# Key and value bias of a slot-attention kernel formed from the unscaled folded weight products, with two weights no longer loaded

## The reference

```python
x_in = _ln(ctx, lnkv_g, lnkv_b)
k = x_in @ wk + bk
v = x_in @ wv + bv
slots = q_mu + jnp.exp(q_logsig) * layernorm(x)
for _ in range(3):
    prev = slots
    q = _ln(slots, lnq_g, lnq_b) @ wq + bq
    attn = softmax(k @ q.T * 16) + 1e-8, normalised over the rows of the context
    slots = (attn.T @ v) @ wu + bu + prev
    slots = gelu(_ln(slots, lnm_g, lnm_b) @ w1 + b1) @ w2 + b2 + slots
    slots = _ln(slots + cond, lnp_g, lnp_b)
x = x + slots
```

## Time and profile before

| what | us |
|---|---|
| median of 3 executions | 339.01 |
| the three | 336.94, 339.01, 339.3 |
| the profiled execution's own time | 339.19 |
| its span, first to last instruction | 337.3 |

### The profile page before, as it was taken

The page is one execution under the profiler, slowest core; times in us unless marked ns, Lnnn a source line. Parts: engine busy times, 40 slices in busy tenths (PEclk is TensorE's granted clock), DMA queues, the critical chain, the costliest instruction groups (busy, mean ns, idle before and its releaser), DMA issues. The chain is left out here.

```text
span 337.3 us, 6560 instructions
## 1 busy us (share of the span) xinstructions
PE 316.9 (94%) x1758; PEld 261.0 (77%) x1758; DVE 292.9 (87%) x851; ACT 235.6 (70%) x563; POOL 202.2 (60%) x385
## 2 busy tenths in 40 slices
PE   8899999999999989999998999799976899999994
PEld 8787888888887878888887788687853577767773
DVE  3699977899899889998999899999998789999874
ACT  2368986967467867785589674855638588898881
POOL 3168966255689764568987547377754944444341
PEclk9999999999999999999999999999999599999999
DMA  7988000000000000000000000000000000000001
GB/s 274 329 320 357 1 1 2 0 0 2 2 0 2 0 2 2 0 3 1 0 2 0 1 2 1 0 3 1 0 2 0 1 34 31 33 31 0 32 34 62
DMA packets 5311, 13.22 MB, mean 39 GB/s; under 512 B 672, under 2 KB 672, under 8 KB 4896
## 3 DMA queue, kind: packets, MB, share of 16 engines
q1 hardware_dynamic: 4160, 10.88, 8.6%
q10 hardware_dynamic: 1120, 1.98, 1.6%
HBM read 10.76 MB, written 2.10 MB: 38 GB/s over the span
## 5 line engine op out<-in xcount | busy, mean ns | idle before, releaser
L290 DVE BATCH_NORM_STATS2 stats<-S 128x6 f32<-128x256 f32 (+1 forms) x112 | 42.0, 416 | 9.3 <-DMA S<-ctx 3.5
L341 PE MATMUL ps_mid<-XT,KT 128*128 128x256 f32 x192 | 46.1, 383 | 3.4 <-ACT XT L357 3.4
L341 PE MATMUL ps_low<-V,PR 128*128 128x257 f32 x192 | 46.2, 383 | 1.7 <-DVE PR L863 1.7
L341 PE MATMUL ps_low<-wn,GT 128*128 128x256 f32 x192 | 45.7, 381 | 0.8 <-ACT GT L639 0.8
L341 PE MATMUL ps_mid<-XT,wt 128*128 128x256 f32 x192 | 45.5, 380 | 0.7 <-ACT XT L357 0.7
L341 PEld LDWEIGHTS ps_low<-V,PR 128*128 128x128 f32 x192 | 36.0, 190 | 8.4 <-DVE PR L863 3.5
L636 ACT ACTIVATE PR<-ps_mid,nmax 128x256 f32<-128x256 f32 x48 | 22.3, 471 | 27.3 <-DVE nmax L873 27.2
L341 PEld LDWEIGHTS ps_low<-wn,GT 128*128 128x128 f32 x192 | 36.1, 190 | 6.7 <-ACT GT L639 1.9
L341 PEld LDWEIGHTS ps_mid<-XT,KT 128*128 128x128 f32 x192 | 34.6, 190 | 8.4 <-ACT XT L357 4.6
L308 POOL TENSOR_TENSOR lnm_ab<-lnm_mv,mhalf 128x2 f32<-128x2 f32 x24 | 17.2, 715 | 38.9 <-DVE lnm_mv L298 38.9
L357 ACT ACTIVATE XT<-ps_t 128x512 f32<-128x512 f32 x56 | 33.1, 591 | 9.2 <-PE ps_t L333 9.2
(11 more groups left out here) (124 smaller groups left out, 706.4 us busy)
## 6 DMA issues: line engine op xcount, KB each, us to landing
S<-ctx SPq DMA_DIRECT2D x8, 256.0 KB, 3.8
X<-x SPq DMA_DIRECT2D x8, 256.0 KB, 3.4
out<-X SPq DMA_DIRECT2D x8, 256.0 KB, 2.0
rowv<-rows SPq DMA_DIRECT2D x1, 1920.0 KB, 9.9
wf<-w_fc_t SPq DMA_DIRECT2D x1, 1024.0 KB, 11.8
wf<-w_proj_t SPq DMA_DIRECT2D x1, 1024.0 KB, 13.8
wt<-w_tr ACTq DMA_DIRECT2D x1, 512.0 KB, 4.2
wn<-w_nat ACTq DMA_DIRECT2D x1, 512.0 KB, 5.8
```

Source lines behind the costliest of these rows:

```text
L290: dve.bn_stats(ln.st[:, at, j, 0:6], tiles[:, j]).then_inc(ln.stats_done, 1)
L341: last = pe.matmul(dst(m), lhs_t[:, c, m * P:(m + 1) * P], rhs[:, c, 0:n], start=(c == 0), stop=(c == 1))
```

## The change

Natural wk and wv are not loaded. ACT, which issued six loads, issues five; SP waits for transposed wv instead of natural wk. ACT copies each of the two products out of PSUM, unscaled, to a new tile `raw`, and DVE folds lnkv_g from there. ACT also spreads lnkv_b and bv over 128 columns each (`spread`, four instructions). All of this stands ahead of ACT's first normalisation. The key bias becomes one accumulation of 8 matmuls, bk with wq and lnkv_b with the raw key product. The value bias becomes one accumulation of 4 matmuls, with the raw value product and wu, and stands in PE's order between the value product and the key product of batch 0. DVE adds bu to it inside batch 0 of the prologue. Two `column` products and the DVE instructions on `ckv` and `bcol` are gone.

```diff
@@ tiles and semaphores
-        wn = sb("wn", [5, C2, D])
+        wn = sb("wn", [3, C2, D])
+        raw = sb("raw", [2, C2, D])
-        bcol = sb("bcol", [C2, P])
+        spread = sb("spread", [2 * C2, P])
-        ckv = sb("ckv", [4, 1])
-        FOLD_CK, FOLD_CV, FOLD_K, FOLD_V, FOLD_ALL = 3, 8, 10, 12, 15
+        FOLD_W, FOLD_K, FOLD_V, FOLD_ALL = 6, 8, 10, 13
@@ sync
-            sp.wait_ge(wk_in, 16)
+            sp.wait_ge(wv_in, 16)
@@ scalar
-            load(wn[:, WK].rearrange("p c d -> p (c d)"), w_nat[0], wk_in)
-            load(wn[:, WV:WU + 1].rearrange("p w c d -> p w (c d)"), w_nat[1:3].rearrange("w p n -> p w n"), wvu_in)
-            load(wt[:, TV].rearrange("p c d -> p (c d)"), w_tr[2], wvu_in)
+            load(wt[:, TV].rearrange("p c d -> p (c d)"), w_tr[2], wv_in)
+            load(wn[:, WU].rearrange("p c d -> p (c d)"), w_nat[0], wu_in)
...
+            def copy_raw(i):
+                act.wait_ge(w_prod, i + 1)
+                act.activation(raw[:, i].rearrange("p c d -> p (c d)"), ps_mid[i][:], ACT.Copy).then_inc(raw_ready, 1)
+
+            act.wait_ge(cols_in, 16)
+            act.wait_ge(consts, 2)
+            for c in range(C2):
+                act.activation(spread[:, c], ones[:], ACT.Copy, scale=col("lnkv_b", c)).then_inc(spread_ready, 1)
+                act.activation(spread[:, C2 + c], ones[:], ACT.Copy, scale=col("bv", c)).then_inc(spread_ready, 1)
+            copy_raw(0)
+            copy_raw(1)
             ln_apply(act, lnc, 0, 0, S[:, 0], XR[:, 0], xc_ready)
@@ vector
-            dve.wait_ge(w_prod, 1)
+            dve.wait_ge(raw_ready, 1)
             for c in range(C2):
-                dve.tensor_scalar(Wkq[:, c], ps_mid[0][:, c * D:(c + 1) * D], col("lnkv_g", c), None,
+                dve.tensor_scalar(Wkq[:, c], raw[:, 0, c], col("lnkv_g", c), None,
                                   ALU.mult).then_inc(w_fold, 1)
-            dve.wait_ge(w_prod, 2)
-            dve.tensor_tensor(ckv[:, 0:2, 0], ps_low[0][:, 0, 0:2], colv[:, COL["bk"]:COL["bk"] + 2],
-                              ALU.add).then_inc(w_fold, 1)
...
+            dve.wait_ge(raw_ready, 2)
+            for c in range(C2):
+                dve.tensor_scalar(Wvu[:, c], raw[:, 1, c], col("lnkv_g", c), None,
+                                  ALU.mult).then_inc(w_fold, 1)
+            rows_x(0, 0)
+            bn_sum(dve, lnx, 0, 0)
             dve.wait_ge(w_prod, 3)
...
-            rows_x(0, 0)
-            bn_sum(dve, lnx, 0, 0)
             dve.wait_ge(bu_in, 16)
-            dve.wait_ge(w_prod, 6)
-            for j in range(J2):
-                dve.tensor_tensor(vbias[:, j], ps_low[1][:, 1, 0:D], row("bu"), ALU.add).then_inc(w_fold, 1)
             dve.wait_ge(sig_ready, 1)
...
+                if isinstance(b, int) and b == 0:
+                    dve.wait_ge(w_prod, 4)
+                    for j in range(J2):
+                        dve.tensor_tensor(vbias[:, j], ps_low[1][:, 1, 0:D], row("bu"), ALU.add).then_inc(w_fold, 1)
+                    dve.wait_ge(w_fold, FOLD_V)
                 dve.wait_ge(low_ready, b + 1)
-                if isinstance(b, int) and b == 0:
-                    dve.wait_ge(w_fold, FOLD_V)
@@ tensor
-            pe.wait_ge(cols_in, 16)
-            pe.wait_ge(wk_in, 16)
-            column(ps_low[0][:, 0], wn[:, WK], lambda c: col("lnkv_b", c)).then_inc(w_prod, 1)
-
-            pe.wait_ge(wvu_in, 32)
+            pe.wait_ge(wv_in, 16)
+            pe.wait_ge(wu_in, 16)
             product(pe, side(ps_mid[1]), wt[:, TV], wn[:, WU]).then_inc(w_prod, 1)
 
-            column(ps_low[0][:, 1], wn[:, WV], lambda c: col("lnkv_b", c)).then_inc(w_prod, 1)
             pe.wait_ge(consts, 5)
             context_t(0, 0)
 
-            pe.wait_ge(w_fold, FOLD_CK)
-            column(ps_low[1][:, 0], wt[:, TQ], lambda c: ckv[:, c]).then_inc(w_prod, 1)
-
-            pe.wait_ge(cv_spread, 2)
-            for c in range(C2):
-                last = pe.matmul(ps_low[1][:, 1, 0:D], bcol[:, c], wn[:, WU, c], start=(c == 0), stop=(c == C2 - 1))
-            last.then_inc(w_prod, 1)
+            pe.wait_ge(cols_in, 16)
+            pe.wait_ge(raw_ready, 1)
+            column(ps_low[1][:, 0], (wt[:, TQ], lambda c: col("bk", c)), (raw[:, 0], lambda c: col("lnkv_b", c)))\
+                .then_inc(w_prod, 1)
+
+            def value_bias():
+                pe.wait_ge(raw_ready, 2)
+                pe.wait_ge(spread_ready, 2 * C2)
+                rhs = [raw[:, 1, c] for c in range(C2)] + [wn[:, WU, c] for c in range(C2)]
+                for i in range(2 * C2):
+                    last = pe.matmul(ps_low[1][:, 1, 0:D], spread[:, i], rhs[i], start=(i == 0), stop=(i == 2 * C2 - 1))
+                last.then_inc(w_prod, 1)
 
             def keys_values(b, u):
                 pe.wait_ge(t_copied, b + (1 + RING))
-                if isinstance(b, int) and b == 0:
-                    pe.wait_ge(w_fold, FOLD_V)
+                if isinstance(b, int) and b < 2:
+                    pe.wait_ge(w_fold, FOLD_K if b else FOLD_W)
                 pe.wait_ge(low_read, 2 * b + 2)
                 product(pe, side(ps_low[u][:, 0]), XT[:, u], Wvu).then_inc(low_ready, 1)
+                if isinstance(b, int) and b == 0:
+                    value_bias()
                 pe.wait_ge(mid_read, 2 * b + 2)
                 product(pe, side(ps_mid[u]), Wkq, XT[:, u]).then_inc(mid_ready, 1)
```

More of the change, by code:

```diff
@@ L118, in col @@
             return colv[:, COL[name] + c:COL[name] + c + 1]
-        WK, WV, WU, W1, W2 = range(5)
+        WU, W1, W2 = range(3)
         TK, TQ, TV = range(3)
@@ L151, in build @@
         wkq_in = sem("wkq_in")
-        wk_in = sem("wk_in")
-        wvu_in = sem("wvu_in")
+        wv_in = sem("wv_in")
+        wu_in = sem("wu_in")
+        raw_ready = sem("raw_ready")
         mlp_in = sem("mlp_in")
@@ L161, in build @@
         w_fold = sem("w_fold")
-        cv_spread = sem("cv_spread")
+        spread_ready = sem("spread_ready")
         sig_ready = sem("sig_ready")
@@ L380, in _ @@
             sp.dma_start(wn[:, W1:W2 + 1].rearrange("p w c d -> p w (c d)"),
-                         w_nat[3:5].rearrange("w p n -> p w n")).then_inc(mlp_in, 16)
+                         w_nat[1:3].rearrange("w p n -> p w n")).then_inc(mlp_in, 16)
             sp.dma_start(rowv[:, ROWS_EARLY:], rows[ROWS_EARLY:].rearrange("(a n) -> a n", a=1)
@@ L680, in _ @@
             dve.wait_ge(cols_in, 16)
-            dve.wait_ge(w_prod, 1)
+            dve.wait_ge(raw_ready, 1)
             for c in range(C2):
-                dve.tensor_scalar(Wkq[:, c], ps_mid[0][:, c * D:(c + 1) * D], col("lnkv_g", c), None,
+                dve.tensor_scalar(Wkq[:, c], raw[:, 0, c], col("lnkv_g", c), None,
                                   ALU.mult).then_inc(w_fold, 1)
-            dve.wait_ge(w_prod, 2)
-            dve.tensor_tensor(ckv[:, 0:2, 0], ps_low[0][:, 0, 0:2], colv[:, COL["bk"]:COL["bk"] + 2],
-                              ALU.add).then_inc(w_fold, 1)
             for c in range(C2):
                 dve.tensor_scalar(kgain[:, c:c + 1], col("lnq_g", c), LOGIT_SCALE, None, ALU.mult).then_inc(w_fold, 1)
-            dve.wait_ge(w_prod, 3)
-            for c in range(C2):
[L692 to L701, removed]
+            dve.wait_ge(raw_ready, 2)
[4 more added lines that the diff above has]
+            bn_sum(dve, lnx, 0, 0)
+            dve.wait_ge(w_prod, 3)
             for c in range(C2):
@@ L743, in w1_fold @@
                     dve.tensor_scalar(W1g[:, c], wn[:, W1, c], col("lnm_g", c), None, ALU.mult).then_inc(w_fold, 1)
-                dve.wait_ge(w_prod, 7)
+                dve.wait_ge(w_prod, 5)
                 dve.tensor_tensor(b1fold[:], ps_low[0][:, 1, 0:2], colv[:, COL["b1"]:COL["b1"] + 2],
@@ L947, in _, with column @@
             pe.sem_inc(mid_ready, RING)
-            def column(dst, w, v):
+            def column(dst, *pairs):
                 for m in range(C2):
-                    for c in range(C2):
-                        last = pe.matmul(dst[:, m:m + 1], w[:, c, m * P:(m + 1) * P], v(c),
-                                         start=(c == 0), stop=(c == C2 - 1))
+                    for i, (w, v) in enumerate(pairs):
+                        for c in range(C2):
+                            last = pe.matmul(dst[:, m:m + 1], w[:, c, m * P:(m + 1) * P], v(c),
+                                             start=(i + c == 0), stop=(i == len(pairs) - 1 and c == C2 - 1))
                 return last
@@ L1008, in _ @@
             pe.wait_ge(low_read, 2 * (B - 1) + 2 * RING)
-            column(ps_low[0][:, 1], wn[:, W1], lambda c: col("lnm_b", c)).then_inc(w_prod, 1)
+            column(ps_low[0][:, 1], (wn[:, W1], lambda c: col("lnm_b", c))).then_inc(w_prod, 1)
             def rows_t(b, u):
@@ L1154 @@
         "ctx": g["ctx_1024"],
-        "w_nat": np.stack([tiles(xc[n]) for n in ("wk", "wv", "wu", "w1", "w2")]),
+        "w_nat": np.stack([tiles(xc[n]) for n in ("wu", "w1", "w2")]),
```

## The result

The changed kernel takes 343.37 us, the kernel before 339.07 (4 executions each): a ratio of 1.0134, 95% interval 1.01 to 1.0167. Forecast were 340.2 us and a range of 337.8 to 342.6. The direction was right, the size was not: the median lies 0.8 us above the range. The profiled execution took 343.53 us with a span of 341.6, 4.3 more than before.

A forecast was written before the change was run, and what follows sets the result against it. DVE was taken to pace the prologue, so its shift at V of batch 0 reaches the end: the profiled 339.19 plus 1.05 us gave 340.2 us. The range was 337.8 to 342.6 us.

The forecast's parts named there:

- What bounds it: Prologue: DVE sets the pace at 4.16 us a batch, so a shift at V of batch 0 shifts the end.
- The base, +1.05 us: Set-up: DVE takes V of batch 0 at 18.6 instead of 17.55 us, passed on to the end; chance 0.42.
- The loads' gain: Set-up on PE: smaller loads let the second product start at 7.5 to 8.0 instead of 8.81, 0.8 to 1.3 us.
- ACT's queue: Set-up: spreads and copies ahead of batch 0's normalisation eat the loads' 1.3 us; only 0.15 us is left.
- PE's value bias: Set-up: four matmuls instead of two, usable only at 17.75 us, so DVE, there at 16.85, stands 0.9 us.
- the clock stays where it was: Set-up: the forecast case adds no time for a fall of PE's clock; 340.2 us, chance 0.42.
- 16 one-column matmuls with weight loads fill 1.9 us of the stretch: Set-up on PE: argument against a clock fall, with no row showing whether these matmuls hold the clock.
- The stretch to come: Set-up: PE has no full product from about 9.4 to 14.1 us, only transposes, one-column matmuls and a 1.8 us wait.
- the rival: Set-up: PE's clock falls to half, up to 2.3 us more, time 341.4 to 342.5, middle 341.9; chance 0.28.
- The late stretch: Into the feed-forward: the half-rate stretch does not come, saving 2.2 us, time 338.0; chance 0.18.
- Absorbed: Prologue: PE's or ACT's order sets the pace, so a shift of 0.4 us arrives, time 339.6; chance 0.12.

The follow-up runs named there:

- fill_both: Changed kernel plus seven matmuls of ones before the first transposes and ten where PE waits for DVE in the feed-forward: 338.18 us, ratio 0.9996.
- fill_one_col: Changed kernel plus seven matmuls of ones, one moving column each, on PE between the second product and the first transposes: 342.22 us, ratio 1.013.
- changed_again: The changed kernel run again unaltered, six executions in another set, against the kernel before: 341.7 us, ratio 1.0096.
- bias_early_late: Changed kernel plus late feed-forward fillers, ACT normalising both batches early, value bias ahead of value product, key column behind it: 336.66 us; with four DVE memsets 336.16.

## Why the prediction was wrong

*What bounds it: right.* DVE's V of batch 0 was the place to watch. Its shift of 4.2 us in the first profile was 3.8 at the start of the rounds, and DVE's late hole, here at 233 us, brought it back to 4.25 at the first fc matmuls, for an end 4.3 us later.

*The base, +1.05 us: right in its steps.* The loads' gain was worked out as 0.8 to 1.3 us and came out as 0.7 to 1.2. ACT's queue ate it: the order alone costs 1.6. PE's value bias was DVE's last wait, with 0.9 us worked out and 1.07 measured, and V of batch 0 was 0.97 late in fill_both. What reached the rounds was 0.48, since a hole of some 0.4 us in DVE's stream between V of batches 0 and 1 was not there any more; the profiled executions differ by 0.9 and the medians by 1.46. I had not reckoned with holes of that kind.

*The failing step: that the clock stays where it was.* The sum carried no term for it, and the forecast went to the case in which it holds, 0.42 against 0.28. What spoke for that, "16 one-column matmuls with weight loads fill 1.9 us of the stretch", was the open point, and fill_one_col answers it: with more of these in the gap the clock fell too. The one fall with work behind it in the trace of before came after 3 us with transposes and waits only. The stretch to come was 4.7 us by my own working, so the rival should have been the forecast. What stands in place of the missing term: the clock was at half for 6.8 us in the first profile and for 3.4 in that of changed_again, which put V of batch 1 back by 3.2 and by 1.5 us. The rival had given 2.2 to 3.3 us over the kernel before. The second median, 341.7, is 3.3 above it in its set, at that upper end; the first, 343.37, is 4.3 above and outside.

*The rival's size was too small for the first profile as well.* Its upper end was 2.3 us, half of 4.6 us of products, for 342.5 at most. Measured there was more. V of batch 1 was at 25.46 in the changed kernel and at 22.28 in fill_both, 3.2 us apart. The clock was low for 6.8 us and not from the first product on: it fell at 12.8 us, so the key column and the transposes of batch 1 ran at half rate first (0.99 for 0.58, 1.09 for 0.66), and the value product began 0.9 us later than worked out, at 14.99 instead of 14.1. It came back at 19.6, 4.6 us behind that start, the length that I had taken; but the low stretch had begun 2.2 us ahead of the product, and since changed_again had the clock back 2.3 us behind its start (15.11 to 17.4), that the length came out is luck. The Trainium skill, TensorE: Matmul & The Clock Gate, "HAM oscillation — how this bites in real kernels", says that waits between bursts of matmuls bring the array to half rate. The stretches of the changed kernel agree in part: the clock fell between two products, but PE waited for only 1.7 of the 3.2 us ahead of the fall, and in fill_one_col for 0.25 us ahead of the transposes. The sum that the prediction gave with this rule, 341.9, was 1.5 us below the first median and 0.2 above the second.

*The late stretch: right.* Its 2.2 us agree with the two profiled executions (339.19 and 337.0). As a rival it did not come: the changed kernel had that fall too in its profile. *Absorbed*: no.

What stays open is how often the clock falls in set-up, when, and for how long: the first four executions of the changed kernel had a median of 343.37 us, six more in another set 341.7. Both profiles have the fall, one of twice the length of the other. A profile shows only one execution each.

## What to carry to other kernels

When a change moves a product, or queues what PE waits for behind other work, look at the longest stretch in which PE has only waits, transposes and one-column matmuls. If it is as long as one ahead of which the trace shows the clock falling, the fall deserves the larger chance, and it is paid by all that stands behind it on PE, small instructions too. It is a chance and no more: the clock fell after 3.2 us in one execution here and held through 2.9 in another, and one kernel lost 3.2 us by it in one profile and 1.5 in the next. Matmuls on junk in such a gap are cheap to try. And four spreads and two copies ahead of a normalisation in ACT's fixed order cost more here, about 1.6 us, than leaving out half a megabyte of loads had brought, 0.7 to 1.2.

## What was not expected

Adding PE work made both kernels faster: 14 records of 1.7 us in set-up took 2 to 4 us off the changed kernel's medians, ten matmuls took 1.7 us (338.43 to 336.72) off the median of the old one. DVE has holes of 0.3 to 0.4 us ahead of instructions that wait for no other engine, and the one near 229 us came and went with four instructions in its stream (0.49 us in the ten profiles with 847, 0.15 in the four with 851): the four memsets cost no time, and in bias_early_late the median with them was 0.5 us lower, on another chip.
